# Where the normalised rows of an attention step are split and turned, and in which slots values and queries are computed

## The reference

```python
x = x + xattn(layernorm(x), ctx, ctx, proj_q, bias_q, proj_k, bias_k, proj_v, bias_v, w_out)
    # q = LN(x) Wq + bq;  k, v likewise of ctx;  softmax(q k^T / 8) v;  heads side by side @ w_out.T
x = x + ffn(layernorm(x), w_gate, w_up, w_down)
    # fp4_linear(silu(fp4_linear(x, w_gate)) * fp4_linear(x, w_up), w_down)
```

## Time and profile before

| | |
|---|---|
| median of 3 runs | 409.79 us |
| profiled execution | 407.99 us, span 406.1 us |
| busy in the span | PE 82%, DVE 76%, ACT 65%, POOL 62% |
| start to slot 0 | about 0 to 31 us |
| 64 slots | about 31 to 250 us |
| feed-forward part | about 258 to 406 us |
| granted clock of PE, mean | 0.975 of full speed |
| transposing DMAs `turn` | 70, median 4.1 us from issue to landing |

### The profile page before, as it was taken

How to read it: one execution, slowest core, us unless ns; L and a number is a source line. 1 busy time by engine, 2 the same in 40 slices (tenths; PEclk the granted TensorE clock), 3 DMA queues, 4 the chain that set the end, 5 groups by cost and what they waited for, 6 DMA issues and landing times.

```text
span 406.1 us, 9531 instructions
## 1 busy us (share of the span) xinstructions
PE 334.3 (82%) x3595; PEld 255.8 (63%) x3595; DVE 307.4 (76%) x634; ACT 264.3 (65%) x635; POOL 252.8 (62%) x248
## 2 busy tenths in 40 slices
PE   1778678888988979889798685888759999999976
PEld 1455466566776867768676564566537776676764
DVE  1989658446877758677689766388999999999692
ACT  3767969668898998989898876335423454443431
POOL 7362435528787887877977666247663776776510
PEclk9999789999999999999999989699989999999999
DMA  7991537565889978999898788311000000000001
GB/s 212 321 335 34 98 66 123 105 89 96 138 137 174 146 138 138 150 170 139 154 135 170 136 127 145 61 28 28 13 1 15 26 15 16 24 15 25 17 26 40
DMA packets 125375, 40.86 MB, mean 101 GB/s; under 512 B 117452, under 2 KB 123280, under 8 KB 125329
## 3 DMA queue, kind: packets, MB, share of 16 engines
q1 hardware_dynamic: 125329, 40.25, 51.4%
HBM read 8.78 MB, written 2.10 MB: 27 GB/s over the span
## 4 chain that ended last, share of the span: by engine, by line
DVE 43%; PE 30%; issue 11%; ACT 10%; POOL 3%; DMA 2%; SPq 0%; ACTq 0%; DVEq 0%
PE ps L562 5%; DVE arena L1148 5%; PE ps L483 4%; ACT arena L831 4%; PE ps L617 4%; DVE arena L1150 4%; DVE arena L1102 4%; PE ps L485 3%; PE ps L484 3%; DVE negmax L1071 3%; DVE arena L1273 3%; DVE arena L1087 3%; DVE arena L1239 2%; PE ps L578 2%; POOL arena L1344 2%
## 5 line engine op out<-in xcount | busy, mean ns | idle before, releaser
L1344 POOL TENSOR_TENSOR arena<-arena 128x640 f16<-128x640 f32 x64 | 94.7, 1480 | 71.7 <-ACT arena L841 71.6
L831 ACT ACTIVATE arena<-ps,negmax 128x154 f32<-128x154 f32 x256 | 78.7, 401 | 8.4 <-DVE negmax L1071 7.4
L1071 DVE TENSOR_REDUCE negmax<-ps 128x4 f32<-128x616 f32 x64 | 50.9, 796 | 26.3 <-PE ps L617 26.2
L562 PE MATMUL ps<-v_h,pT 128*128 128x132 f16 (+1 forms) x640 | 52.4, 213 | 16.4 <-DVE arena L1087 8.8
L562 PEld LDWEIGHTS ps<-v_h,pT 128*128 128x128 f16 x640 | 38.7, 99 | 22.7 <-issue 21.3
L483 PE MATMUL ps<-arena 128*128 128x256 f16 (+1 forms) x144 | 41.1, 286 | 10.8 <-DVE arena L976 5.8
L1349 POOL TENSOR_TENSOR arena<-arena 128x256 f16<-128x256 f32 x64 | 44.2, 692 | 7.3 <-ACT arena L848 7.3
L841 ACT ACTIVATE arena<-arena 128x640 f16<-128x640 f32 x64 | 47.9, 748 | 1.1
L483 PE MATMUL ps<-arena,xnT_even 128*128 128x352 f16 x128 | 40.7, 318 | 5.3 <-DVE xnT_even L1158 5.3
L484 PE MATMUL ps<-arena 128*128 128x256 f16 (+1 forms) x144 | 41.0, 285 | 0.0
L485 PE MATMUL ps<-arena 128*128 128x256 f16 (+1 forms) x144 | 40.9, 284 | 0.0
(11 more groups left out here) (155 smaller groups left out, 951.5 us busy)
## 6 DMA issues: line engine op xcount, KB each, us to landing
out_dram<-arena SPq DMA_DIRECT2D x16, 128.0 KB, 1.7
pT<-arena SPq DMA_TRANSPOSE x70, 4.1
xs<-in_x_dram SPq DMA_DIRECT2D x2, 512.0 KB, 7.3
arena<-in_L_xattn_w_out_dram SPq DMA_DIRECT2D x1, 1024.0 KB, 11.8
xs<-in_x_dram SPq DMA_DIRECT2D x2, 384.0 KB, 6.6
wffn<-in_L_ffn_w_down_dram SPq DMA_DIRECT2D x1, 704.0 KB, 9.6
wffn<-in_L_ffn_w_gate_dram SPq DMA_DIRECT2D x1, 640.0 KB, 7.9
wffn<-in_L_ffn_w_up_dram SPq DMA_DIRECT2D x1, 640.0 KB, 8.6
```

The lines of the kernel that those rows point to most:

```text
L562: last = pe.matmul(o[:, h0 * HB:h1 * HB], pT[:, n % RING_P, part * CHUNKS + c], v[:, b, j, at[0]:at[-1] + 1].rearrange("p m k -> p (m k)") ...
L831: last = act.activation(prob[:, j, k * LP:k * LP + L], ps[:, 2 * (j % 2) + k % 2, (k // 2) * L:(k // 2 + 1) * L], ACT.Exp, bias=negmax[:, ...
L1071: dve.tensor_reduce(negmax[:, s, 4 * j:4 * j + 4].rearrange("p (k u) -> p u k", k=2), v, AX.X, ALU.max, negate=True).then_inc(max_done, 1)
L1344: pool.tensor_tensor(part_of(j, 1), prob[:, j], part_of(j, 0), ALU.subtract).then_inc(p_low, 1)
```

## The change

Rows of steps 2 to 7 are no longer turned by PE. ACT normalises them (`rows_normal`) with the columns already sorted by parity, and splits off the high part in SBUF (`rows_high`); POOL makes the low part (`rows_low`), SP issues a transposing DMA of eight blocks (`turn_rows`) straight into `xnT_even` or `xnT_odd`. The task `x` remains for steps 0 and 1 only. The factor 1/8 moves into the reciprocal deviation of LayerNorm (one more DVE instruction in each of two passes, `LN_ROWS`), and the later LayerNorm passes stay without it. `xnT_*` is laid out by tile, part, column half.

The places in the order of slots change too: normalising of step 1 is in slot 3 (4 before) and DVE ends its LayerNorm pass in slot 2; rows of step 2 are made in slot 5, of step i from 3 on in slot 8(i-1)-6; step 2's queries come two pairs at a time in slots 10, 12, 14 and 16; the second batch's values in 11, 13, 15 and 17; `add_attention` stands directly behind the row maximum, ahead of values' low parts and `scale_hid`.

```diff
         def values_at(b, n):
-            return n if b == 0 else 10 + n
+            return n if b == 0 else 11 + 2 * n
 ...
         def rows_at(i):
-            return 5 if i == 1 else 8 * (i - 1) - 1
+            return 3 if i == 1 else 5 if i == 2 else 8 * (i - 1) - 6
 ...
         def query_at(i, p):
-            return 6 + p // 2 if i == 1 else 8 * (i - 1) + 1 + p
+            return 6 + p // 2 if i == 1 else 8 * (i - 1) + (2 if i == 2 else 1) + p
 ...
         def pairs_of(i):
-            return 2 if i <= 1 else 1
+            return 2 if i <= 2 else 1
 ...
-            out += [("x", i) for i in range(1, STEPS) if rows_at(i) == n]
+            out += [("x", 1)] if n == 5 else []
 ...
+            def turn_rows(i):
+                sp.wait_ge(rows_lo, i - 1)
+                if i >= 2: sp.wait_ge(task_mm, TASK_AT[query_tasks(i - 2)[-1]] + 1)
+                sp.dma_start_transpose(rows_turned(i).rearrange("p s a c n -> p (s a c) n"),
+                                       xsplit.rearrange("p s a n -> p (s a n)")).then_inc(rows_done, 16)
 ...
             for n in range(SLOTS + HID_LAG):
                 turn(n)
+                for i in range(2, STEPS):
+                    if rows_at(i) == n: turn_rows(i)
 ...
             def query(i, p0):
-                pe.wait_ge(task_low, TASK_AT[("x", i)] + 1)
+                if i < 2:
+                    pe.wait_ge(task_low, TASK_AT[("x", i)] + 1)
+                else:
+                    pe.wait_ge(rows_done, 16 * (i - 1))
 ...
+            def rows_normal(i):
+                if i >= 3: act.wait_ge(rows_lo, i - 2)
+                if i == 2: act.wait_ge(task_mm, TASK_AT[("x", 1)] + 1)
+                for s in range(B):
+                    last = act.activation(xn[:, s].rearrange("p (c d) -> p d c", c=KC),
+                                          xs[:, s, i].rearrange("p (d c) -> p d c", c=KC), ACT.Identity,
+                                          bias=ln[:, SHIFT, s * STEPS + i:s * STEPS + i + 1],
+                                          scale=ln[:, RSTD, s * STEPS + i:s * STEPS + i + 1])
+                last.then_inc(xn_ready, 1)
+
+            def rows_high(i):
+                act.wait_ge(xn_ready, i + 1)
+                if i >= 3: act.wait_ge(rows_done, 16 * (i - 2))
+                act.activation(xsplit[:, :, 0], xn, ACT.Copy).then_inc(rows_hi, 1)
 ...
                 for r in range(1, STEPS):
-                    if rows_at(r) - (1 if r == 1 else 2) == n: normalised(xn, r, xn_ready)
+                    if rows_at(r) == n:
+                        rows_normal(r)
+                        if r >= 2: rows_high(r)
 ...
+                    if t1 - t0 != EARLY and t0 != EARLY: done(dve.tensor_scalar(r[RSTD], r[RSTD], XS, None, ALU.mult))
 ...
                 row_max(n)
+                if m == (PROJ_LAG + 8) % 8 and n >= PROJ_LAG + 8: add_attention((n - PROJ_LAG - 8) // 8)
                 if n >= 1:
                     for t in tasks_of(n - 1):
                         if t[0] != "q": low(t)
                 if i == 0: first(n)
-                if m == (PROJ_LAG + 8) % 8 and n >= PROJ_LAG + 8: add_attention((n - PROJ_LAG - 8) // 8)
 ...
                 if n == 1:
                     dve.wait_ge(stats_done, 2 * STEPS)
-                    layernorm(1, STEPS, LN_STEPS, [0, 1])
-                if n == 2: layernorm(1, STEPS, LN_STEPS, [2, 3])
-                if n == 3: layernorm(1, STEPS, LN_STEPS, [4])
+                    layernorm(1, STEPS, LN_ROWS, [0, 1])
+                if n == 2: layernorm(1, STEPS, LN_ROWS, [2, 3, 4])
 ...
+            def rows_low(i):
+                pool.wait_ge(rows_hi, i - 1)
+                pool.tensor_tensor(xsplit[:, :, 1], xn, xsplit[:, :, 0], ALU.subtract).then_inc(rows_lo, 1)
 ...
                 if n >= HEADS_LAG + 2: low_hid(n - HEADS_LAG - 2)
+                for r in range(2, STEPS):
+                    if rows_at(r) == n - 1: rows_low(r)
```

More of the change, by code:

```diff
@@ L586, in turn_x @@
                 o = next_task(("x", i))
-                v = xn.rearrange("p s (d c) -> p s c d", c=KC)
-                for c in range(KC):
-                    for s in range(B):
-                        last = pe.transpose(o[:, (2 * c + s) * P:(2 * c + s + 1) * P], v[:, s, c], ident[:, :])
+                for s in range(B):
+                    for c in range(KC):
+                        last = pe.transpose(o[:, (2 * s + c) * P:(2 * s + c + 1) * P], xn[:, s, c * P:(c + 1) * P], ident[:, :])
                 last.then_inc(task_mm, 1)
             def query(i, p0):
-                pe.wait_ge(task_low, TASK_AT[("x", i)] + 1)
+                if i < 2:
+                    pe.wait_ge(task_low, TASK_AT[("x", i)] + 1)
+                else:
+                    pe.wait_ge(rows_done, 16 * (i - 1))
                 o = next_task(("q", i, p0))
@@ L679, in gate_up @@
                     for c in range(KC):
-                        last = three(ps[:, m, 0:GU], xnT_h[:, c, s * P:(s + 1) * P], xnT_l[:, c, s * P:(s + 1) * P],
+                        last = three(ps[:, m, 0:GU], xnT_even[:, s, 0, c], xnT_even[:, s, 1, c],
                                      w1_h[:, c, m * GU:(m + 1) * GU], w1_l[:, c, m * GU:(m + 1) * GU],
@@ L861, in normalised @@
                 for s in range(B):
-                    last = act.activation(dst[:, s], xs[:, s, bass.ds(i, 1), :].rearrange("p o d -> p (o d)"), ACT.Identity,
+                    last = act.activation(dst[:, s], xs[:, s, i], ACT.Identity,
                                           bias=ln[:, SHIFT, bass.ds(s * STEPS + i, 1)],
@@ L938, in ffn @@
                     if exists(summed[0]): y_copy(*summed)
[L939 removed]
+                    if peeled(i, LATE - 3) and s == 1: act.wait_ge(ln_step, 2 * LN_ROWS + 2 * LN_STEPS)
                     if s == 1 and exists(i + 2): magnitude_x(i + 2)
@@ L1123, in x_low @@
             def x_low(i):
-                h, l = (rows_turned(i)[:, part].rearrange("p c t -> p (c t)") for part in range(2))
-                dve.scalar_tensor_tensor(l, task_out(("x", i)), XS, h, ALU.mult, ALU.subtract).then_inc(task_low, 1)
+                h, l = (rows_turned(i)[:, :, part].rearrange("p s c n -> p s (c n)") for part in range(2))
+                dve.tensor_tensor(l, task_out(("x", i)).rearrange("p (s n) -> p s n", s=B), h, ALU.subtract).then_inc(task_low, 1)
             def low(t):
@@ L1157, in xq_low @@
                 dve.wait_ge(xqt_high, 2 * i + s + 1)
-                dve.scalar_tensor_tensor(xnT_l[:, :, s * P:(s + 1) * P], ps[:, XT_BANK, 0:D].rearrange("p (c t) -> p c t", c=KC),
-                                         -1.0, xnT_h[:, :, s * P:(s + 1) * P], ALU.mult, ALU.subtract).then_inc(xqt_low, 1)
+                h, l = (xnT_even[:, s, part].rearrange("p c t -> p (c t)") for part in range(2))
+                dve.scalar_tensor_tensor(l, ps[:, XT_BANK, 0:D], -1.0, h, ALU.mult, ALU.subtract).then_inc(xqt_low, 1)
             def minus_grid_w(w, half):
```

33 lines of the change are left out of this document (17 added, 16 removed).

## The result

The change makes the kernel faster, by about a quarter of what was forecast (3.9 us for 15.1): 406.0 us median (404.38 to 407.5, ten runs) against 409.94 of the kernel before on the same chip (407.39 to 413.1, ten runs). The ratio is 0.9896, interval 0.9858 to 0.9933. Forecast were 394.7 us with a range of 390.0 to 402.5; the time is outside it, the direction is right. The profiled span went from 406.1 to 404.2 us.

The account below looks back on a forecast made before the run. After the change ACT, at 22.4 us a step against PE's 21.6, was taken to bound the kernel. Gains of 11.0, 3.4 and 1.1 less 0.4 sum to 15.1 us, giving 394.7 us, range 390 to 402.5.

Parts of the forecast that it names:

- The middle steps: Four steps, slots 19 to 51: 21.8, 22.4, 22.4 and 22.0 us, a gain of 11.0 us.
- the lag of ACT: From slot 19 ACT may fall about 1.4 us behind before PE feels it, filled in slot 26.
- ACT's sum: ACT's work in a middle step: plain slots 20.3, filler L890 0.5, rows 1.5; 22.3 us, 22.4 with one stretched slot.
- the spread output: Rival: ACT's normalising writes neighbours 512 bytes apart, making a middle step 0.44 us longer; 396.0 us, chance 0.10.
- PE alone at 21.6: Middle steps: PE by itself would need 21.2 + 0.4 = 21.6 us a step.
- The wait in m = 2 of 0.4: Middle steps: of PE's 0.69 us lost for `add_attention` in m = 2, and handing over, 0.4 remain.
- GpSimd or ACT takes the room: Rival, middle steps: POOL makes `scale_hid` late or ACT's slots lengthen; steps of 23.8, 401.3 us, chance 0.22.
- Slots 3 to 6: Early slots: PE's own part of step 1's rows done earlier and at full clock, +1.1 us, bounds -1 and 3.
- The start: Rows of step 0 pass a longer DVE chain with a spread output: -0.4 us, bounds -1 and 0.
- Slots 8 to 19: PE's bank waits go as task kinds alternate, less new waits: +3.4 us together, between 0 and 6.
- The 39 to 40 of the signs: Sign of being right: about 39 to 40 us from slot 8's row maximum to slot 18's.
- L883 at 0.84: Sign of being wrong: ACT's L883, the normalising, above 0.7 us each.

Follow-up runs that it names:

- e3: Changed kernel with DVE's LayerNorm pass spread over slots 2 and 3 and ACT's normalising of step 1 back in slot 4: 401.68 us, ratio 0.9793.
- e4: Changed kernel with ACT's normalising of steps 1 to 7 writing in order and reading every second element: 405.34 us, ratio 0.9872.
- e9: Changed kernel with ACT's work on rows of steps 3 to 7 cut to 16 of 256 elements, the rest left out: 401.67 us.
- e13: Changed kernel with ACT's rows of steps 3 to 7 cut to 16 of 256 elements and VectorE's grid pieces to 64 of 704 columns: 397.76 us.
- e18: e17 with ACT's magnitude of the weights' piece in m = 4 also cut to 64 of 704 columns: 401.24 us.
- e17: e13 with VectorE's block scales of the weights also cut to 4 of 44 blocks from the second slice on: 399.42 us.

## Why the prediction was wrong

- **The middle steps, the step that failed first**: "I take 21.8 for the first step, 22.4 for the next two, and 22.0 for the last". Measured are 23.95 to 23.99 in all four, a gain of 3.73 for 11.0. The first would have been 22.88 at full clock, as in e3, so there the lag of ACT did leave room, 1.1 us of it. The working took each engine's own sum and let the larger one set the step. Two things were wrong in it.
  - *ACT's sum was too small.* From start to start the rows were priced at 1.69 (1.5 once the 0.17 that a filler hides is taken off); they take 2.02, and 1.70 in e4. So the miss is the spread output, 0.32 a step, a rival of the prediction that came true at three quarters of its price. A plain slot is 2.56, not 2.54. Eight of these, 1.87 for the rows (2.02 less the 0.15 that they hide) and 0.51 for L919 are 22.9, not 22.3. Cutting ACT's work took its length off the step nearly one for one (1.08 of 1.14), so this sum does count.
  - *Stalls come on top of the sum.* The step is 1.1 us longer than ACT's sum, and that was put at nothing. The same 1.1 stands in e4 (23.65 over 22.5) and in e9 (22.88 over 21.7), however much work ACT has. Of it, 0.64 are ACT's two recorded waits for a row maximum. By the cuts, VectorE's pieces account for 0.26 (0.31 in e13 against e9) and its block scales for 0.2; the rest is not traced to a cause. The cuts add: ACT's rows -1.08, VectorE's pieces -0.26, both -1.39. That a plain slot of 2.56 on ACT beside 2.65 on PE leaves no room to win a stall back is my reading of this.
- **PE alone at 21.6**: not reached in the later steps, neither with ACT's rows and the pieces cut (22.57) nor in e18 (22.19); 21.71 in the first step of e17. The wait in m = 2 of 0.4 was right (0.42); the one for `q_low` behind the block scales (0.61 in e13) was not seen. The trace of before has none at that place: PE's waits there are the three of the earlier trace rows in m = 7, 0 and 2.
- **"GpSimd or ACT takes the room"**, steps of 23.8 and 401.3 us, came near in the step (23.96) and not in the time (406.0). Its reasons bear little of it: GpSimd's subtraction took 1.16 (forecast 1.15) and costs 0.1 a step at most, `scale_hid` waits for GpSimd in three slots a step (0.32, 0.86, 0.82) where before it did in two (0.47, 0.83), and ACT's plain slots are hardly longer. So that its 23.8 is close is partly luck.
- **Slots 3 to 6, +1.1 with bounds of -1 and 3**: from slot 2 to 8 the loss is 3.6 us. The prediction named LayerNorm whole in slot 2 and counted it as a shift. It is a chain of small instructions ahead of a row maximum for which PE and ACT wait, and GpSimd's subtractions held it for 1.8 us more (0.63 + 1.20). With the order repaired the loss goes (e3: 22.50 from slot 2 to 8, for 23.16 before and 26.75 after; 3.0 less on average over all traces). Nor was PE's part done at full clock: the four transposes of the rows, at 50.03 us, took 1.12 as before, in a longer stretch at the lower level.
- **The start, -0.4**: slot 0 was at 32.41 for 31.69, -0.7. In other runs with the same start it was at 31.77 to 35.09, so this isn't told from scatter.
- **Slots 8 to 19, +3.4**: right, 3.66, or 4.1 at full clock. Slots 8 to 18 took 38.0 us. The 39 to 40 of the signs don't fit the working, whose own terms up to slot 18 (5.8 + 2.0 - 1.5 - 0.7 = 5.6 off 44.04) give 38.4. PE's wait at the head of slot 18 for the values' low part is there, in the timeline of the kernel after:

```profile
107.53 0.40 PE L572 MATMUL ps<-v_h,pT 128*128 128x66 f16 x5 [2.38 <-DVE v_l L1060]
```

- **Signs named beforehand**: no wait for `xnT` (right), 0.3 to 0.5 for L1124 (0.41, right), no wait for `rows_done` (right), 2 us at slot 18 (2.38, right), ACT without idle time (not quite, waits of 0.64 a step), steps of 22 (wrong). Of the signs against it one showed fully, L883 at 0.84, and the steps ended just below its 24 us.
